# A fused attention and feed-forward layer: four more row units beside the feed-forward, four half steps without one, and the last up projection between the first and the second score pair

## The reference, cut to what matters

```
xn  = layernorm(x)                                  # x: 1024 tokens x 512
q, k, v = bitnet_linear(xn, Wq | Wk | Wv)           # sign(W) times a row scale; q 32 heads, k and v 8 heads of 16
out = softmax(q k^T / 4) v                          # each k/v head serves 4 q heads
ffn = (silu(xn Wg^T) * (xn Wu^T)) Wd^T              # inner width 1792, weights ternary times a scale
y   = x + bitnet_linear(out, Wo) + ffn
```

## Time and profile before

| what | value |
| --- | --- |
| median of three executions | 501.98 us (500.68 to 502.21) |
| the profiled execution | 501.71 us, of which the span is 500.0 us |
| TensorE, VectorE, ScalarE, GpSimd busy | 96%, 83%, 70%, 20% of the span |
| feed-forward stage ends, softmax stage begins | at 152.0 us of the span |
| steps 0 to 107 | 152.0 to about 398.8 us |

### The profile page before, as it was taken

How to read it: one execution, slowest core, us unless ns; L and a number is a source line. 1 busy time by engine, 2 the same in 40 slices (tenths; PEclk the granted TensorE clock), 3 DMA queues, 4 the chain that set the end, 5 groups by cost and what they waited for, 6 DMA issues and landing times.

```text
span 500.0 us, 10314 instructions
## 1 busy us (share of the span) xinstructions
PE 480.1 (96%) x4171; PEld 163.6 (33%) x4171; DVE 415.7 (83%) x487; ACT 348.1 (70%) x640; POOL 101.7 (20%) x154
## 2 busy tenths in 40 slices
PE   1899999999998999999999999999999999999996
PEld 0564444433332222222222222222222233333442
DVE  7879868676777999999999999999999955223986
ACT  1943543352228999999999999999999978774000
POOL 4212334534424011011011011001101213241021
PEclk9999999999998999999999999999999999999999
DMA  8853783642103812212212312222221133453321
GB/s 263 266 109 84 165 163 41 182 93 24 22 0 40 152 25 42 64 25 43 64 24 44 65 39 47 43 55 34 42 64 25 15 108 94 102 156 86 105 83 45
DMA packets 64424, 39.28 MB, mean 79 GB/s; under 512 B 39729, under 2 KB 53937, under 8 KB 64377
## 3 DMA queue, kind: packets, MB, share of 16 engines
q1 hardware_dynamic: 55352, 27.59, 22.6%
q0 software_dynamic: 8304, 10.95, 11.8%
q10 hardware_dynamic: 720, 0.08, 0.1%
HBM read 33.37 MB, written 10.48 MB: 88 GB/s over the span
## 4 chain that ended last, share of the span: by engine, by line
PE 93%; DVE 3%; ACT 2%; DMA 1%; issue 1%; SPq 0%; ACTq 0%; DVEq 0%
PE ps L1309 28%; PE ps L1144 19%; PE ps L1247 14%; PE ps L1153 11%; PE ps L1217 5%; PE ps L1204 5%; PE ps L1125 4%; PE ps L1339 3%; PE ps L1278 2%; ACT room L718 2%; DMA hlo<-x 1%; DVE stats L777 1%; DVE room L799 1%; PE ps L1117 1%; DVE room L804 0%
## 5 line engine op out<-in xcount | busy, mean ns | idle before, releaser
L853 DVE TENSOR_REDUCE nmx<-ps 128x1 f32<-128x1024 f32 x248 | 283.2, 1216 | 13.4 <-PE ps L1153 13.2
L718 ACT ACTIVATE room<-ps 128x512 f32<-128x512 f32 x512 | 271.1, 598 | 20.5 <-PE ps L1278 11.5
L1309 PE MATMUL ps<-room,vcur 128*32 128x256 f32 (+1 forms) x1880 | 159.8, 412 | 0.3 <-ACT room L718 0.3
L1153 PE MATMUL ps<-kA,qst 48*128 48x512 f16 x496 | 139.3, 384 | 0.0
L1247 PE MATMUL ps<-qst,kB 50*128 50x512 f16 x432 | 134.8, 384 | 1.3 <-ACT room L718 1.3
L1144 PE MATMUL ps<-room,wf 128*128 128x512 f16 x448 | 100.6, 379 | 0.0
L1309 PEld LDWEIGHTS ps<-room,vcur 128*32 128x32 f32 x1880 | 37.2, 108 | 95.0 <-issue 52.1
L699 ACT ACTIVATE room<-ps,gsc 128x512 f32<-128x512 f32 x28 | 19.2, 686 | 62.4 <-PE ps L1144 62.4
L1144 PEld LDWEIGHTS ps<-room,wf 128*128 128x128 f16 x448 | 42.4, 98 | 55.1 <-issue 7.2
L1247 PEld LDWEIGHTS ps<-qst,kB 50*128 50x128 f16 x432 | 28.3, 93 | 97.0 <-ACT room L718 84.6
L562 POOL TENSOR_SCALAR mxs<-mxs 16x128 f32<-16x128 f32 x16 | 8.3, 520 | 214.8 <-DMA mxs<-m_scratch 214.6
(11 more groups left out here) (137 smaller groups left out, 316.9 us busy)
## 6 DMA issues: line engine op xcount, KB each, us to landing
qst<-q_scratch SPq DMA_DIRECT2D x32, 192.0 KB, 3.6
o_scratch<-osb SPq DMA_DIRECT2D x16, 256.0 KB, 2.5
q_scratch<-parts SPq DMA_DIRECT2D x12, 256.0 KB
hlo<-x SPq DMA_DIRECT2D x8, 256.0 KB, 5.3
parts<-x POOLq DMA_DIRECT2D x8, 256.0 KB, 3.7
wf<-gate POOLq DMA_DIRECT2D x14, 128.0 KB, 3.8
wf<-up POOLq DMA_DIRECT2D x14, 128.0 KB, 5.9
wd<-down POOLq DMA_DIRECT2D x1, 1792.0 KB, 13.9
```

Source lines behind the costliest of these rows:

```text
L718: nc.scalar.activation(probs[:, s % 2, r, :], ps[:, bank_of(step, i), :], ACT.Exp, scale=gam_reg[par][r]).then_inc(scores_free, 1)
L853: nc.vector.tensor_reduce(nmx[:, hf, idx:idx + 1], bank_pair(idx % 2), AX.X, ALU.max, negate=True).then_inc(rows_free, 1)
L1153: return nc.tensor.matmul(ps[:, 2 * (idx % 2) + b, :], qst[low:low + KROWS, par, hf, head, qt * P:(qt + 1) * P], kA[low:low + KROWS, par, ...
L1309: mm = nc.tensor.matmul(ps[32 * r:32 * r + 32, value_bank(step_ // TT), of], vcur[:, par, key_tile(r, j), :], probs[:, s % 2, r, of], star ...
```

## The change

Six things are edited.

1. The tables now hold units A0 to A35 on TensorE and VectorE, instead of A0 to A31, and place them earlier: two after nearly each piece from F6 on. `AHEAD` = 4 is the number of units by which the softmax stage is ahead.
2. Four half steps of the softmax stage, numbers 27, 81, 135 and 189 of 216 (`SINGLE`), have no row unit. `unit_of` numbers the others, so that step 0 begins with unit 36 where it began with unit 32, and the last unit before step 108 is 247 in both.
3. TensorE's table ends with G26, G27, A34, A35, U26 (gate 26, gate 27, two units, up projection 26), where it ended with F26, A30, A31, F27.
4. Up projection 27 follows the first score pair of step 0: `scores(0, 0, range(2))`, then `feed_forward(27, 1)`, then the second pair.
5. ScalarE, after silu 27, loads the exponential table, runs the exponentials of the first pair, then casts piece 26, waits for up projection 27, and runs the second pair's.
6. The exponentials of the first pair of step 0 are put in the room of the weight buffers `wf` (`early_probs`), since those of `probs` still hold the normalized input that up projection 27 reads.

```diff
-    pe_order = ("... F24 A26 A27 F25 A28 A29 F26 A30 A31 F27 ")
+    pe_order = ("... F24 A30 A31 F25 A32 A33 G26 G27 A34 A35 U26 ")
-    dve_order = ("... F25 A29 F26 A30 A31 F27 ")
+    dve_order = ("... F25 A32 A33 F26 A34 A35 F27 ")
+    AHEAD = 4
+    SINGLE = [(2 * i + 1) * LATE // AHEAD for i in range(AHEAD)]
+    def unit_of(step, pair):
+        place = 2 * step + pair
+        if place in SINGLE:
+            return None
+        return 2 * UNITS + AHEAD + place - sum(p < place for p in SINGLE)
...
-            act.wait_ge(up_ready, FU)
-            exps(0, 0, False)
+            exps(0, 0, False, range(REP // 2))
+            hidden_high(FU - 2)
+            act.wait_ge(up_ready, FU)
+            exps(0, 0, False, range(REP // 2, REP))
             hidden_high(FU - 1)
...
-                    idx = 2 * j + i // 2
-                    if i < REP - 1:
+                    unit = unit_of(gp * 2 * STEPS + s, i // 2)
+                    if unit is not None and i < REP - 1:
                         if i % 2 == 0:
-                            pe.wait_ge(rows_free, (gp_ * 2 + par + 1) * (2 * UNITS) + hf * UNITS + idx + 1)
-                        mm = half_rows(1 - par, hf, idx, 1 - half)
+                            rows_loaded(unit)
+                            pe.wait_ge(rows_free, unit + 1)
+                        mm = half_rows(unit, 1 - half)
...
-            pe.wait_ge(h_ready, FU - 1)
             pe.wait_ge(kones_ready, 2)
-            scores(0, 0, opening=True)
+            scores(0, 0, range(REP // 2))
+            feed_forward(FU - 1, 1)
+            scores(0, 0, range(REP // 2, REP))
```

More of the change, by code:

```diff
@@ L79, in layer_kernel @@
     assert pe_order.index(("F", SPLIT_AT)) > pe_order.index(("A", UNITS - 1))
-    assert [n for kind, n in pe_order if kind in "FU"] == list(range(FU))
+    assert [n for kind, n in pe_order if kind in "FU"] == list(range(FU - 1))
     assert dve_order.index(("A", SUM_AT - 1)) < dve_order.index(("S", 1)) < dve_order.index(("A", SUM_AT))
@@ L83, in layer_kernel @@
     for order in (pe_order, dve_order):
-        assert [n for kind, n in order if kind == "A"] == list(range(2 * UNITS))
+        assert [n for kind, n in order if kind == "A"] == list(range(2 * UNITS + AHEAD))
     assert [n for kind, n in act_order if kind == "F"] == list(range(FU))
@@ L252, in layer_kernel, with probs_of @@
         rsum = sb("rsum", [P, QT + 1, T // D], F32)
+        def probs_of(step, r):
+            if step == 0 and r in EARLY:
+                return early_probs[:, EARLY.index(r), :]
+            return probs[:, step % 2, r, :]
         x_loaded = [sem(f"x_loaded{i}") for i in range(TT)]
@@ L700, in _ @@
                                          scale=gsc[:, f:f + 1]).then_inc(gt_ready, 1)
-                    if n >= 1:
+                    if 1 <= n < FU - 1:
                         hidden_high(n - 1)
@@ L707, in load_scale, with exps @@
                 act.reg_load(gam_reg[par][r], gam_words[0:1, bass.ds(g * REP + r, 1)])
-            def exps(gp, s, last):
+            def exps(gp, s, last, entries=range(REP)):
                 gp_, par, hf, j = at(gp, s)
@@ L715, in exps @@
                 act.wait_ge(probs_free, step + 1)
-                for i, r in enumerate(ROUND):
+                for i in entries:
+                    r = ROUND[i]
                     act.wait_ge(scores_ready, step * REP + i + 1)
-                    nc.scalar.activation(probs[:, s % 2, r, :], ps[:, bank_of(step, i), :], ACT.Exp,
+                    nc.scalar.activation(probs_of(step, r), ps[:, bank_of(step, i), :], ACT.Exp,
                                          scale=gam_reg[par][r]).then_inc(scores_free, 1)
@@ L966, in _ @@
                 elif kind == "A":
-                    row_max(n, n // UNITS, n % UNITS)
+                    row_max(n, n // UNITS % 2, n % UNITS)
             def step_rows(gp, s, last):
-                gp_, par, hf, j = at(gp, s)
                 step = gp * (2 * STEPS) + s
-                ga_ = gp_ * 2 + par + 1
                 if step < LATE:
-                    row_max(ga_ * (2 * UNITS) + hf * UNITS + 2 * j, hf, 2 * j)
-                    row_max(ga_ * (2 * UNITS) + hf * UNITS + 2 * j + 1, hf, 2 * j + 1)
+                    for pair in range(2):
+                        n = unit_of(step, pair)
+                        if n is not None:
+                            row_max(n, n // UNITS % 2, n % UNITS)
                 elif step < ROWS_END:
@@ L1147, in feed_forward, with half_rows @@
                 mm.then_inc((gate_ready, up_ready)[z], 1)
-            def half_rows(par, hf, idx, b):
+            def half_rows(n, b):
+                par, hf, idx = n // (2 * UNITS) % 2, n // UNITS % 2, n % UNITS
                 head, qt = idx // (HALF // P), idx % (HALF // P)
@@ L1155, in half_rows, with rows_loaded, rows @@
                                         kA[low:low + KROWS, par, :], start=True, stop=True)
-            def rows(n, par, hf, idx):
+            def rows_loaded(n):
+                g, hf = n // (2 * UNITS), n // UNITS % 2
+                if n % UNITS == 0:
+                    pe.wait_ge(q_loaded[g % 2][hf], 32 * (g // 2 + 1))
+                if n % (2 * UNITS) == 0:
+                    pe.wait_ge(kA_loaded[g % 2], 32 * (g // 2 + 1))
+            def rows(n):
                 pe.wait_ge(rows_free, n + 1)
-                half_rows(par, hf, idx, 0)
-                half_rows(par, hf, idx, 1).then_inc(rows_ready, 1)
+                half_rows(n, 0)
+                half_rows(n, 1).then_inc(rows_ready, 1)
             def transpose_last_max():
@@ L1185, in _ @@
                         pe.wait_ge(kA_loaded[0], 32)
-                    if n % UNITS == 0:
-                        pe.wait_ge(q_loaded[0][n // UNITS], 32)
                     if n == SUM_AT:
                         pe.wait_ge(factors_ready, 3)
-                    rows(n, 0, n // UNITS, n % UNITS)
+                    rows_loaded(n)
+                    rows(n)
             def down_strips(i, f, part):
@@ L1220, in down_proj, with scores @@
                     mm.then_inc(down_ready, 1)
-            def scores(gp, s, opening=False):
+            def scores(gp, s, entries=range(REP)):
                 gp_, par, hf, j = at(gp, s)
@@ L1244, in scores @@
                         pe.wait_ge(scores_free, 3 + last_use[gp * 2 * STEPS + s, i])
-                    if opening and i == 0:
+                    if s == 0 and i == 0:
                         pe.wait_ge(gt_ready, FU)
+                    if s == 0 and i == 2:
+                        pe.wait_ge(h_ready, FU - 1)
                     nc.tensor.matmul(ps[:, score_bank(block_, e), :],
@@ L1257, in scores @@
                         if i == REP - 2:
-                            half_rows(1 - par, hf, idx, half).then_inc(rows_ready, 1)
-                    if i % 2 == 1 and not opening:
+                            half_rows(unit, half).then_inc(rows_ready, 1)
+                    if i % 2 == 1 and s > 0:
                         times_values(gp, s - 1, i // 2, 2)
@@ L1309, in times_values @@
                     mm = nc.tensor.matmul(ps[32 * r:32 * r + 32, value_bank(step_ // TT), of], vcur[:, par, key_tile(r, j), :],
-                                          probs[:, s % 2, r, of], start=(j == 0 and part == 0),
+                                          probs_of(step_, r)[:, of], start=(j == 0 and part == 0),
                                           stop=(j == TT - 1 and part == cut - 1))
```

9 lines of the change are left out of this document (6 added, 3 removed), and 6 rows, old and new, of the table dve_order.

## The result

| | median | runs | ratio to before |
| --- | --- | --- | --- |
| before | 502.2 us | 14, 500.3 to 505.4 | |
| the change | 505.85 us | 14, 503.5 to 509.0 | 1.0071 [1.0052, 1.009] |

The forecast was 502.5 us and no difference that can be told; the range ended at 504.2. The profiled execution took 506.87 us, its span 505.1 against 500.0.

What follows compares the result with a forecast made beforehand. TensorE was taken to bound the feed-forward stage, VectorE the softmax blocks (18.10 us, TensorE 18.04 behind). +1.3 for units and opening, -0.5 for steps 2 to 108, make +0.8: span 500.8, time 502.5 us, range 501.0 to 504.2.

Steps and rivals of the forecast that it cites:

- A: Likeliest case: the whole kernel at full clock ("clock full throughout"), 502.5 us, own range 501.3 to 503.3; chance 0.46.
- B: Rival: clock falls to 0.50 in the new opening waits, costing +1.0 to +1.7 us, 1.5 taken; 503.9 us; chance 0.32.
- 1.73 us of dense matmuls: Argument against a clock fall: up projection 27's matmuls follow the first new wait, where before there were short groups.
- Units before the softmax, +0.98 us: Feed-forward stage: 17 pairs and 2 single units instead of 14 and 4 take TensorE 9.82 us, not 8.84.
- The two waits: Opening: TensorE idles some 1.85 us before unit 36, then from 156.3 to 157.75 before unit 38, for VectorE's reductions.
- +1.3 us: Delay at step 2's second half: 0.98 from units, 0.3 by which new waits exceed the old wait and low clock.
- The old low clock: Kernel before, between the stages: clock at 0.50 until 159.6 lengthens two half steps by 0.83 + 0.69 = 1.5 us.
- Rival C: Opening: reductions don't hold TensorE and the early pair pays, 1.8 us less than before, 499.4 us; chance 0.12.
- Steps 2 to 107, "I take -0.5": Softmax stage up to step 108: four fewer VectorE units let TensorE set the pace, saving 0.5 us.
- eleven blocks: Softmax stage: blocks go from VectorE's 18.10 us to TensorE's 18.04, 11 x 0.06 = 0.7 us at most.
- the half steps without a unit themselves: Four softmax half steps: scores starting together save 0 because exponentials hold the next products; bounds 0 and 0.9 us.
- Rival D: Softmax stage: VectorE's four omitted units count in full, up to 4.5 us less, about 498.8 us; chance 0.03.

Runs made afterwards that it cites:

- all seven later ones: The changed kernel, nothing edited, timed again in a later set beside the two best variants: 506.9 us, ratio 1.008 to before.
- filling its hole: Kernel before, with six superfluous full-array matmuls between the third and fourth score of step 0: 501.64 us, ratio 0.9979.
- The filled waits: Changed kernel with superfluous matmuls in its two TensorE waits, 8 ahead of unit 36's first matmul and 4 ahead of unit 38's: 503.59 us, ratio 1.0019.
- the units-only kernel: Kernel before with only four more units in the feed-forward stage and four half steps without one, opening sequence as before: 503.16 us, ratio 1.0022.
- the reordered kernel: Changed kernel with only up projection 27 moved behind the first score pair, 32 units in the feed-forward stage as before: 506.09 us, ratio 1.0071.

## Why the prediction was wrong

**The step that failed** is "The forecast: 502.5 us, clock full throughout", chance 0.46, against B, "The clock falls in the new waits", chance 0.32. The low clock was the rule: 10 of the change's 14 executions had a mean clock of 0.997 or less, and so had all seven later ones. I had weighed "the new gap is longer" against "behind it stand 1.73 us of dense matmuls"; the dense matmuls were just what ran at half clock. B was also sized too small: it had one fall of 1.5 us, and "the second wait" only as something that hides a part. In the profile the second wait brought a fall of its own: 1.6 us for the first, 1.5 us for the second. With the forecast's own other terms two falls make 502.5 + 3.1 = 505.6; that this is near the measured 505.85 is in part luck, since the 502.5 is itself about 1 us low. The filled waits show the cause: same waits, work in them, 2.3 us less in the median, 2.6 by the ratios to the before of each set.

**The clock is not all of it.** The three executions of the change with a mean clock of 0.999 or 1.000 took 503.5 to 503.7 us, and A, "clock full throughout", had 501.3 to 503.3. In the profiles 0.6 us are the start (below) and 0.4 us the last part, -0.1 measured for -0.5.

**Units before the softmax, +0.98 us.** Right: +1.1 in the table of stretches.

**The two waits.** Right in place, releaser and size: 1.85 and about 1.45 us put down (151.5 to 153.35, 156.3 to 157.75), 1.72 and 1.28 shown idle. "+1.3 us" for units and opening together took the old low clock as gone and no new one as come. At full clock that holds: the opening's part was 10.00 less 1.83 = 8.17 against 7.80, +0.4 for the forecast +0.3. The old low clock was put at 1.5 us; filling its hole gave 1.24. Rival C, "the early pair pays", was not what happened, but is what the kernel does once three reductions stand elsewhere: 7.06 us in place of 7.80 + 1.83 = 9.63 up to the second half of step 2. The waits, not the early pair, were the fault.

**Steps 2 to 107, "I take -0.5".** Right in sign, wrong in its reason. From the second half of step 2 to the last half step before 108 it was 237.39 us before (159.81 to 397.20) and 237.05 in the change (165.06 to 402.11): -0.3. The -0.5 stood on eleven blocks at TensorE's 18.04 us in place of VectorE's 18.10. Those did not come. The change's output copies (answers to the earlier trace rows) stand 18.05 us apart once, right behind the first block with an omitted unit, and then again as before, 234.02 - 215.92 = 18.10:

```profile
215.92 0.58 ACT L751 COPY osb<-ps 128x512 f32<-128x512 f32 x1
...
234.02 0.58 ACT L751 COPY osb<-ps 128x512 f32<-128x512 f32 x1
```

VectorE as the limit was read rightly, but an omitted unit relieves it only on the spot. It idles 0.6 to 1.0 us there, since the next unit's matmuls are not done, and from then on its reductions stand 1.13 us apart without a gap again: (60.05 - 1.22) / 52 = 1.131 us in the second row of VectorE in the units-only kernel above, and 60.05 us for 53 in the change too. What was won came from the half steps without a unit themselves, for which the forecast had 0: three blocks with one are 17.96 us. The change's TensorE around half step 27:

```profile
189.75 0.42 PE L1278 MATMUL ps<-qst,kB 50*128 50x512 f16 x2
190.10 0.64 PE L1341 MATMUL ps<-room,vcur 128*32 128x256 f32 x8
190.67 0.39 PE L1278 MATMUL ps<-qst,kB 50*128 50x512 f16 x1
...
191.89 0.39 PE L1278 MATMUL ps<-qst,kB 50*128 50x512 f16 x1
```

The half step without a unit takes 0.92 us, its two scores together, as the Trainium skill's rule on row groups has it (TensorE: Matmul & The Clock Gate, Part 3); the trace agrees. The next takes 1.22 instead of 1.11 while the products wait for the exponentials. Of 0.19 us 0.11 are given back, so 0.08 stay, for a forecast 0. Half steps 135 and 189 go the same way (0.93 and 0.92, then 1.21 and 1.22). Half step 81 does not: it falls on the one of 1.41 us in its block and takes 1.41 without a unit too. Rival D is refuted by the units-only kernel; its 498.8 was counted from the median, and from the 501.7 of the sum it would have been 498.5.

**The starting point.** The profiled execution of before had reached the first key projection at 22.70 us, the change's at 23.33, with nothing changed ahead of it: 0.6 us of the 5.1 are no effect of the change. In the twelve profiles this point lies at 22.42 to 24.57 us, and 22.70 is the second lowest: that the forecast was made against one execution counted for that much.

## What to carry to other kernels

When a step is moved on one engine, look in the table of the engine that answers to it for what now stands ahead of the answer: here two reductions, and later a third, sat ready behind products that could not start. With only the reordering, moving three reductions up turned a loss of 3.5 us into a gain of 1.6 and 1.7 us against the before of each set (the second not clear of noise); with the four more units too, it turned 3.6 us into no difference that can be told. In this kernel a wait of TensorE had two prices, its length and the low clock that followed in some executions; price the second for each wait, and take the likeliest case with it. To separate the two, put superfluous matmuls into the wait: its length stayed, and the share of executions with a mean clock of 0.999 or more went from 3 of 14 to 10 of 12.

## What the runs showed of the hardware

Idle pieces as short as 1.28 to 1.72 us were followed by 3.4 us at 0.50 of the clock. The wait of 1.7 to 1.8 us was so followed in two of the three profiles that have it, and the full-array matmuls behind it did not prevent that: they ran at half clock, 0.43 us each in place of 0.23 (up projection 27, 3.42 us against 1.84 for eight). The wait of 1.1 to 1.3 us ahead of unit 38's matmul (unit 32's in the reordered kernel) was so followed in two of four. So whether the clock falls differs from one execution to the next of one kernel, at the same waits: 3 of the change's first 14 executions had a mean of 0.999 or 1.000 and took 503.5 to 503.7 us, with a median of 505.85 over all.
